# Attention and routed experts on one core: the sums of values in two PSUM banks by turns, six banks in place of seven for scores and dense stages

## The chip, the cores and the metric

The kernel runs on one core of a Trainium2 chip. The metric is the time of one launch on the device in microseconds (us), as the median of several runs. Engines are named as in the profile: PE is TensorE's matmul, PEld its weight load, DVE is VectorE, ACT is ScalarE, POOL is GpSimd, SP is SyncE, whose queue issues the DMAs.

## What is computed

The input is x of shape (2, 2048, 256). It passes two blocks, each followed by a layer norm over x plus the block's result:

```python
x = layernorm(x + windowed_attention(x))      # windows of 128, keys of the window and the one before
x = layernorm(x + ffn_block(x))
```

The second block holds most of the work. Its attention is causal over rows of x, with 16 heads of 16 columns, and its values then go to a layer of eight experts of which each row takes two:

```python
scores = einsum('bqhd,bkhd->bhqk', q, k) * scale      # q, k from x with rotary embedding
scores = where(causal, scores, -inf)
attn   = softmax(scores, axis=-1)
ctx    = einsum('bhqk,bkhd->bqhd', attn, v)
x1     = layer_norm(x + ctx @ out_proj_w.T + out_proj_b)
gates  = softmax(x1 @ gate_w.T + gate_b)              # the two largest of 8 are kept
moe    = sum over the two of gate * (x1 @ expert_w[e].T + expert_b[e])
x2     = layer_norm(x1 + moe)
```

## The kernel before

**Tiles and jobs.** The 4096 rows are 32 tiles of 128 (T in the code). The causal attention is cut into 40 jobs (J, `JOBS`): a job is four heads by two or four query tiles, and has 2 to 16 tiles of keys (`key_tiles`). For each job PE makes the scores twice. Steps `mx` (lines 1369 to 1377) put queries by keys into a PSUM bank, and DVE reduces it to row maxima (step `mr`, line 1065). From these come the negated maxima, split in three bf16 parts, transposed (`nm_T`, line 1382), copied by ACT and stored by SP as extra rows of the query operand (`nm_st`, line 806). Steps `st` (lines 1397 to 1406) then put keys by queries, with the maxima already subtracted, into a bank, and ACT takes the exponential into a ring of 16 SBUF slots (`ex`, line 978, `pbuf`). Steps `pv` (line 1424) multiply values by these exponentials, with the sums of rows as a 17th column. One `pv` step is one tile of keys, four heads beside each other on four quarters of the partitions, and it adds into one bank, `obank`, over all the key tiles of the job. Four `pv` steps of a job run without anything between them (`VRUN = 4`). After the job's last one ACT copies the bank to SBUF (`o_evac`, line 958 with `osb` as output), PE transposes it (`o_T`, line 1430), and DVE divides by the sums (`oden`, line 1109, and line 1119).

**Dense stages.** Around the jobs run, tile by tile, steps named by their first letter: `a_` for the windowed attention, `r_` for rotary embedding, projections and stores, `d_` for the output projection and norm, `f_` for the gate and the experts (`f_e0` to `f_e3` are four matmul groups of two experts each, line 1537; DVE reads `f_e0` and `f_e2` at lines 1296 and 1299, ACT reads `f_e1` and `f_e3`), `g_` for the last norms. `w_` and `load_` steps are weights and loads; `w_rows` (lines 1099 and 1100) sets a row of ones and clears `obank`.

**Banks.** PSUM has eight banks of 128 x 512 f32. Seven (`BANKS`, line 175) are shared by `mx`, `st` and every step of a dense stage that PE writes. `obank` is the eighth. Each shared bank has two semaphores, `filled[b]` and `emptied[b]`; PE waits for `emptied[b]` before the first matmul of a step, and the engine that reads the bank adds to it.

**What sets the order.** The function `plan` is a list scheduler that runs on the host when the program is built. Each step has an engine, a cost in ns, a rank (lower is more urgent) and a list of steps before it. Time after time it takes the step that can start earliest, ties by rank, gives a bank-writing step the bank that came free first, and writes down one order, which every engine's queue then follows. A kind of step can hold only so many banks at a time:

```python
BANKS = 7
SHARE = {"mx": 3, "st": 3, "stage": 4}
...
                if step[0] in EMPTIES:
                    kind = kind_of(step)
                    if not free or taken[kind] == SHARE[kind]:
                        continue
                    start = max(start, min(free)[0])
```

The first `pv` step of a run of four needs the exponentials of these four key tiles, the values of the group, and in the list `("o_evac", J - 1)`. In the program the first `pv` of job J waits with `pe.wait_ge(osb_ready, J)`, which is that the copy of the job before is done; the first job waits for the cleared bank instead.

Of the kernel before, what the change touches and what calls it, by code (L numbers as in the profile page):

```python
# [14 lines left out]
P = 128  # L15
# [4 lines left out]
DV = DH + 1  # L20
# [19 lines left out]
PB = VRUN * HJ  # L40
# [131 lines left out]

BANKS = 7
SHARE = {"mx": 3, "st": 3, "stage": 4}


# [156 lines left out]
def job_steps():  # L335

    rows = {}
    turn = [GT * place(J) + GT * (J - last_job(place(J)) - 1) / sum(place(x) == place(J) for x in range(NJ)) + GT
            for J in range(NJ)] + [GT * NG]

    def add(name, J, engine, ns, rank, *before):
        rows[name, J] = engine, ns, rank, [x for x in before if x[1] >= 0]

    for J in range(NJ):
        (s, hg, j0, nj), nk, length = JOBS[J], key_tiles(J), turn[J + 1] - turn[J]
        r, newest = turn[J], GT * s + j0 + nj - 1
        for c in range(keys_groups(J)):
            back = [("pv", J - 1, min(GT * c + GT, key_tiles(J - 1)) - 1)] if J and GT * c < key_tiles(J - 1) else [("pv_end", J - 2)]
            add(f"vload{c}", J, "SP", 500, r + 0.3 * length, ("vstore", newest), *back)
        n = len(mx_list(J))  # L350
        for i, (c, j, h, heads, cols) in enumerate(mx_list(J)):
            diag = c == s % GB
            rows["mx", J, i] = ("PE", heads * max(cols / 2.4 + 3, 98) + (220 if cols == P else 95 * heads) * diag, r + length * i / n,
                                [(f"kh{hg}{k}" if s == GB else f"kst{k}", newest) for k in range(3)] +
                                [(f"qst{k}", LATE.index(newest)) for k in range(3)])
            rows["mr", J, i] = ("DVE", heads * cols / 0.96 + 55, r + length * i / n,
                                [("mx", J, i)] + ([("nm_a", J - 1)] if J else []))
        add("nm_a", J, "DVE", 130, r - 1, ("nm_e", J - 1), *[("mr", J, i) for i in range(n)])
        for a, b in zip("bcde", "abcd"):
            add(f"nm_{a}", J, "DVE", 100, r - 1, (f"nm_{b}", J), ("nm_T", J - 1))  # L360
        add("nm_T", J, "PE", 100, r - 1, ("nm_e", J))
        add("nm_Tc", J, "ACT", 200, r - 1, ("nm_T", J), ("nm_st", J - 1))
        add("nm_st", J, "SP", 1300, r - 1, ("nm_Tc", J))
        r, n = turn[J + 1], len(st_list(J))
        for i, (kb, h, heads, cols) in enumerate(st_list(J)):
            diag = kb - first_diag(J) >= j0
            rows["st", J, i] = ("PE", heads * max(cols / 2.4 + 3, 98) + (220 if cols == P else 95 * heads) * diag, r + length * i / n,
                                [("nm_st", J), ("ones", 0)] + [("ones_later", 0)] * (s > 0))
            back = [("pv", *key_tile_at(key_tiles_before(J) + kb - VRUN))] if key_tiles_before(J) + kb >= VRUN else []
            rows["ex", J, i] = ("ACT", heads * cols * 0.833 + 68, r + length * i / n,  # L370
                                [("st", J, i)] + back + [("st0", 1), ("r_vst", 1)] * (J == i == 0))
        for kb in range(nk):

            lo, hi = st_tiles(J, kb)
            cols = (hi - lo) * P
            first, last = kb // VRUN * VRUN, min(kb // VRUN * VRUN + VRUN, nk) - 1
            rows["pv", J, kb] = ("PE", cols * 4 / 2.4 + 10 + (170 if kb == first else 0), r + length * (st_last(J, last) + 1.5) / n,
                                 [("ex", J, i) for i in range(st_last(J, last) + 1)] + [(f"vload{kb // GT}", J)] +
                                 ([("o_evac", J - 1)] if J else []) if kb == first else [("pv", J, kb - 1)])
        add("pv_end", J, "PE", 0, r + 1, ("pv", J, nk - 1))  # L380
        freed = GT * (place(J) - 2) + GT - 1
        add("o_evac", J, "ACT", 495, r + length / 2, ("pv", J, nk - 1), ("o_T", J - 1))
        add("o_T", J, "PE", 440, r + length / 2, ("o_evac", J), ("d_cT", freed))
        add("o_den", J, "DVE", 120, r + length / 2, ("o_T", J))
        add("o_ctx", J, "DVE", 340, r + length / 2, ("o_den", J), ("d_cT", freed))
    return rows
# [77 lines left out]
def build(nc, windows, cs, w_qk_t, w_out, in_t, in_b, wo_t, gate_t, exp_t, exp_b, rows, gate_b, out):  # L464
# [6 lines left out]
    with ExitStack() as ctx:  # L471
# [47 lines left out]
        vcur = sb("vcur", [P, TB, HJ, DV])  # L519
        pbuf = sb("pbuf", [P, PB, GQ])  # L520
# [5 lines left out]
        osb = sb("osb", [P, GQ])  # L526
# [74 lines left out]
        assert small_taken <= 358  # L601

        bank = [ctx.enter_context(nc.psum_tensor(f"bank{i}", [P, 512], F32)) for i in range(8)]
        obank = bank[BANKS]

        def ps(*step):
            return bank[use[step][0]]
# [16 lines left out]
        consts, rows_set, scaled = sem("consts"), sem("rows_set"), sem("scaled")  # L624
# [6 lines left out]
        osb_ready, oden_ready = sem("osb_ready"), sem("oden_ready")  # L631
# [324 lines left out]
        def _(act):  # L956
            def copy(o, i, scale=1.0):
                return nc.scalar.activation(o, i, ACT.Copy, scale=scale)  # L958

            for step in order:  # L960
# [6 lines left out]
                if name == "ex":  # L967
                    J, i = step[1:]
                    kb, h, heads, cols = st_list(J)[i]
                    nj = JOBS[J][3]  # L970
                    u0 = ((key_tiles_before(J) + kb) * HJ + h) % PB
# [13 lines left out]
                elif name == "nm_Tc":  # L985
                    J = T
# [3 lines left out]
                    nj = JOBS[J][3]  # L990
                    rows_nm = NPART * nj * HJ
                    copy(nmT[0:rows_nm, :], bk[0:rows_nm, 0:P // 2].bitcast(BF16)).then_inc(emptied[b], 1)
                elif name == "o_evac":
                    J = T
# [1 line left out]
                    if J:  # L996
                        act.wait_ge(*fill("o_T", J - 1))
                    nj = JOBS[J][3]
                    copy(osb[:, 0:nj * P], obank[:, 0:nj * P]).then_inc(osb_ready, 1)
                elif name == "a_xTc":  # L1000
                    act.wait_ge(*fill("a_xT", T))
                    copy(xT[e], bk[:, :].rearrange("p (c t) -> p c t", c=EC)).then_inc(emptied[b], 1)
# [46 lines left out]
        def _(dve):  # L1049
            v = nc.vector  # L1050
            for step in order:
# [6 lines left out]
                if name == "mr":  # L1058
                    J, i = step[1:]
                    c, j, h, heads, cols = mx_list(J)[i]  # L1060
# [7 lines left out]
                elif name == "nm_a":  # L1068
                    g, nj = keys_groups(T), JOBS[T][3]
# [7 lines left out]
                elif name in ("nm_b", "nm_c", "nm_d", "nm_e"):  # L1077
                    nj = JOBS[T][3]
# [18 lines left out]
                        v.tensor_tensor(part[2], rest, part[1], ALU.subtract).then_inc(nmp_ready, 1)  # L1097
                elif name == "w_rows":
                    v.memset(ones[:, 0, :], 1.0).then_inc(rows_set, 1)
                    v.memset(obank[:, :], 0.0).then_inc(rows_set, 1)  # L1100
                elif name == "w_scale":
                    dve.wait_ge(in_loaded, 32)
                    v.tensor_scalar(inw[:, :, 0:E], inw[:, :, 0:E], DH ** -0.5, None, ALU.mult).then_inc(scaled, 1)
# [1 line left out]
                elif name == "o_den":  # L1105
                    nj = JOBS[T][3]
# [3 lines left out]
                elif name == "o_ctx":  # L1110
                    s, hg, j0, nj = JOBS[T]
# [5 lines left out]
                    u0 = (pos % 2) * GT + j0  # L1117
# [220 lines left out]
        def _(pe):  # L1338
            mm, tr = nc.tensor.matmul, nc.tensor.transpose
            k_known = 0  # L1340
            pe.wait_ge(consts, CONSTS)
            for step in order:
# [7 lines left out]
                if name == "mx":  # L1350
                    J, i = step[1:]
                    s, hg, j0, nj = JOBS[J]
                    pos = place(J)
                    c, j, h, heads, cols = mx_list(J)[i]
# [16 lines left out]
                    for x in range(heads):  # L1371
                        head = hg * HJ + h + x
                        last = mm(bk[:, x * cols:(x + 1) * cols].rearrange("p (n t) -> p n t", t=P),  # L1373
                                  qs5[0:KR, pos % QRING, j, head, :], ks5[0:KR, kslot, 0:cols // P, head, :],
                                  start=heads < HJ, stop=x == HJ - 1 or not diag)
                        if diag and heads < HJ:
                            last = mm(bk[:, x * cols + j * P:x * cols + (j + 1) * P], idb[:, :], maskb[:, :],  # L1377
                                      start=False, stop=True)
# [4 lines left out]
                elif name == "st":  # L1383
                    J, i = step[1:]
                    s, hg, j0, nj = JOBS[J]
                    kb, h, heads, cols = st_list(J)[i]
# [12 lines left out]
                    for x in range(heads):  # L1399
                        head = hg * HJ + h + x  # L1400
                        last = mm(bk[:, x * cols:(x + 1) * cols].rearrange("p (n t) -> p n t", t=P),  # L1401
                                  ks5[0:KR + NPART, kslot, kb % GT, head, :],
                                  qs5[0:KR + NPART, place(J) % QRING, lo:hi, head, :],
                                  start=heads < HJ, stop=x == HJ - 1 or not diag)
                        if diag and heads < HJ:
                            last = mm(bk[:, x * cols:x * cols + P], maskb[:, :], idb[:, :], start=False, stop=True)  # L1406
                    last.then_inc(filled[b], 1)
                elif name == "pv":
                    J, kb = step[1:]
                    nk, nj = key_tiles(J), JOBS[J][3]  # L1410
                    lo, hi = st_tiles(J, kb)
                    r0, r1 = (lo - JOBS[J][2]) * P, nj * P
                    if kb % VRUN == 0:
                        pe.wait_ge(*drain("st", J, st_last(J, min(kb + VRUN, nk) - 1)))
                    u0 = (key_tiles_before(J) + kb) * HJ
                    if kb % GT == 0:
                        pe.wait_ge(vcur_loaded[kb // GT], 16 * (loads_before(J, kb // GT) + 1))
                    if kb == 0:
                        if J:
                            pe.wait_ge(osb_ready, J)  # L1420
                        else:
                            pe.wait_ge(rows_set, 2)
                    for h in range(HJ):
                        last = mm(obank[32 * h:32 * h + DV, r0:r1], vcur[:, kb, h, :], pbuf[:, (u0 + h) % PB, r0:r1],  # L1424
                                  start=kb == 0, stop=kb == nk - 1, tile_position=(0, 32 * h))
                    last.then_inc(pv_done, 1)
                elif name == "o_T":
                    pe.wait_ge(osb_ready, T + 1)
                    for j in range(JOBS[T][3]):
                        last = tr(bk[:, j * P:(j + 1) * P], osb[:, j * P:(j + 1) * P], idf[:, :])  # L1430
# [158 lines left out]
```

## Time and profile before

| | |
|---|---|
| median of 3 runs | 1450.21 us (1449.8 to 1451.3) |
| the profiled execution, its own time | 1447.28 us |
| its span, first to last instruction | 1445.5 us |
| PE busy | 1384.9 us, 96% |
| DVE busy | 1089.6 us, 75% |
| ACT busy | 783.6 us, 54% |
| POOL busy | 428.0 us, 30% |
| DMA queue q1, share of 16 engines | 23.2% |

The span is what the trace covers; 1.8 us of the execution lie around it. A matmul's duration in the trace holds the time until its result is written, so that two matmuls in a row overlap and a short pause between them does not show as idle time of PE. The weight load before a matmul (PEld) has a row of its own, and where a step waits for a semaphore it is most often the load that carries the wait.

### The profile page before, as it was taken

The numbers are of one execution on the slowest core, as the hardware profiler recorded it, in microseconds if no ns is written. First come the engines' busy times: TensorE is split into PE (matmuls) and PEld (weight loads), VectorE is DVE, ScalarE is ACT, GpSimd is POOL, SyncE is SP. The second block draws the span as 40 slices with busy tenths as digits, with TensorE's granted clock in tenths as the row PEclk, the third lists the DMA queues.
The fourth block names the chain that finished last, engine by engine and source line by source line (L and its number), as shares of the span: only waits on it lengthen the run. The fifth ranks groups of instructions, "written<-read, shape, count | busy, mean of one in ns | idle before, by whom it ended". The sixth has DMA issues, their size and how long they took to land.

```text
span 1445.5 us, 28119 instructions
## 1 busy us (share of the span) xinstructions
PE 1384.9 (96%) x9600; PEld 773.2 (53%) x9600; DVE 1089.6 (75%) x2736; ACT 783.6 (54%) x1707; POOL 428.0 (30%) x707
## 2 busy tenths in 40 slices
PE   7899999999999999999999999999999999999995
PEld 6767655554455445354656655555443355555542
DVE  3765877887787887778655897888778787888745
ACT  3235365555665555666655445554656467665651
POOL 4434522322232231122343543333121110111233
PEclk9999999999999999999999999999999999999997
DMA  3865422230211121120116232222120011111100
GB/s 116 201 172 128 124 57 61 58 85 21 63 46 46 38 62 33 40 57 20 50 49 156 79 90 68 57 57 65 29 60 21 22 24 29 33 32 33 34 23 12
DMA packets 152560, 88.57 MB, mean 61 GB/s; under 512 B 114430, under 2 KB 145974, under 8 KB 152163
## 3 DMA queue, kind: packets, MB, share of 16 engines
q1 hardware_dynamic: 152419, 86.78, 23.2%
q8 instruction: 78, 1.28, 0.4%
q14 instruction: 63, 0.52, 0.1%
HBM read 60.71 MB, written 25.43 MB: 60 GB/s over the span
## 4 chain that ended last, share of the span: by engine, by line
PE 44%; DVE 4%; ACT 3%; issue 2%; SPq 2%; DMA 2%; POOL 1%; POOLq 0%; DVEq 0%; ACTq 0%
PE bank L1537 11%; PE bank L1424 10%; PE bank L1401 8%; PE bank L1373 7%; ACT pbuf L978 2%; DVE mxs L1065 2%; SPq L806 1%; DMA qs<-nmT 1%; PE bank L1494 1%; PE bank L1377 1%; PE bank L1406 1%; PE bank L1513 1%; PE bank L1472 1%; PE bank L1480 1%; PE bank L1523 1%
## 5 line engine op out<-in xcount | busy, mean ns | idle before, releaser
L1065 DVE TENSOR_REDUCE mxs<-bank 128x1 f32<-128x512 f32 (+3 forms) x1120 | 709.4, 667 | 150.1 <-PE bank L1373 79.6
L978 ACT ACTIVATE pbuf<-bank 128x512 f32<-128x512 f32 (+1 forms) x1112 | 588.6, 599 | 326.1 <-PE bank L1401 151.0
L1401 PE MATMUL bank<-qs,ks 99*128 99x256 bf16 (+3 forms) x1536 | 420.7, 319 | 16.4 <-DMA qs<-nmT 10.9
L1373 PE MATMUL bank<-ks,qs 96*128 96x512 bf16 (+3 forms) x1280 | 423.0, 349 | 4.9 <-DVE mxs L1065 2.5
L1424 PE MATMUL bank<-pbuf,vcur 128*17 128x256 f32 (+3 forms) x3072 | 253.5, 469 | 0.3
L1401 PEld LDWEIGHTS bank<-qs,ks 99*128 99x128 bf16 x1536 | 142.3, 98 | 172.1 <-issue 56.3
L1537 PE MATMUL bank<-ew,x1T 128*128 128x512 f32 x464 | 222.4, 601 | 0.4 <-DVE mxs L1065 0.3
L1373 PEld LDWEIGHTS bank<-ks,qs 96*128 96x128 bf16 x1280 | 123.3, 98 | 129.7 <-issue 40.6
L1424 PEld LDWEIGHTS bank<-pbuf,vcur 128*17 128x17 f32 x3072 | 79.8, 97 | 147.4 <-issue 109.6
L1537 PEld LDWEIGHTS bank<-ew,x1T 128*128 128x128 f32 x464 | 82.0, 190 | 72.3 <-issue 60.8
L958 ACT ACTIVATE etmp<-bank,small 128x256 f32<-128x256 f32 x116 | 48.7, 471 | 80.1 <-PE bank L1537 80.1
L1377 PE MATMUL bank<-maskb,idb 128*128 128x128 bf16 x384 | 81.4, 220 | 0.0
L927 POOL TENSOR_TENSOR accp<-accp,etmp 128x256 f32<-128x256 f32 x29 | 21.1, 727 | 201.1 <-ACT etmp L958 201.1
L923 POOL TENSOR_TENSOR accp<-etmp 128x256 f32<-128x256 f32 x29 | 21.1, 728 | 188.6 <-ACT etmp L958 188.6
L1406 PE MATMUL bank<-idb,maskb 128*128 128x128 bf16 x352 | 73.6, 220 | 0.0
L1296 DVE SCALAR_TENSOR_TENSOR acc<-bank,small,acc 128x256 f32<-128x256 f32 x58 | 27.9, 480 | 52.7 <-PE bank L1537 52.7
L1494 PE MATMUL bank<-rxT,inw 128*128 128x128 f32 x464 | 57.0, 276 | 0.0
L1494 PEld LDWEIGHTS bank<-rxT,inw 128*128 128x128 f32 x464 | 55.1, 192 | 2.2 <-issue 1.3
L899 POOL CAST parts<-qkf 128x512 bf16<-128x512 f32 x28 | 17.4, 623 | 122.9 <-DVE qkf L1159 122.9
L873 POOL TENSOR_SCALAR small<-small 128x1 f32<-128x1 f32 x32 | 7.1, 223 | 156.5 <-DVE small L1143 156.3
L1377 PEld LDWEIGHTS bank<-maskb,idb 128*128 128x128 bf16 x384 | 37.8, 98 | 13.7 <-issue 8.9
L958 ACT ACTIVATE osb<-bank 128x512 f32<-128x512 f32 (+1 forms) x40 | 20.5, 512 | 43.7 <-PE bank L1424 43.1
(279 smaller groups left out, 1746.2 us busy)
## 6 DMA issues: line engine op xcount, KB each, us to landing
vcur<-v_scratch SPq DMA_DIRECT2D x92, 136.0 KB, 2.3
parts_scratch<-parts SPq DMA_DIRECT2D x29, 384.0 KB, 3.3
xw<-windows SPq DMA_DIRECT2D x29, 256.0 KB, 2.8
qs<-parts_scratch SPq DMA_DIRECT2D x32, 192.0 KB, 3.3
ks<-parts_scratch SPq DMA_DIRECT2D x28, 192.0 KB, 3.4
qs<-parts_scratch SPq DMA_DIRECT2D x32, 128.0 KB, 3.1
v_scratch<-vst SPq DMA_DIRECT2D x29, 136.0 KB, 2.4
x_scratch<-x SPq DMA_DIRECT2D x29, 128.0 KB, 1.7
```

The lines of the kernel that those rows point to most:

```text
L923: pool.tensor_tensor(accp[f], etmp[f][:, 0, :], etmp[f][:, 1, :], ALU.add).then_inc(accp1_ready, 1)
L958: return nc.scalar.activation(o, i, ACT.Copy, scale=scale)
L978: nc.scalar.activation(pbuf[:, u0:u0 + heads, nj * P - cols:nj * P], bk[:, 0:heads * cols].rearrange("p (h t) -> p h t", h=heads), ACT.Exp)\
L1065: v.reduce_max(mxs[:, j * HJ + h:j * HJ + h + heads, c], bk[:, 0:heads * cols].rearrange("p (h t) -> p h t", h=heads), AX_X)\
L1296: v.scalar_tensor_tensor(out=acc[f], in0=bk[:, 0:E], scalar=wts[f][:, 2 * k:2 * k + 1], in1=acc[f], op0=ALU.mult, op1=ALU.add).then_inc(ha ...
L1373: last = mm(bk[:, x * cols:(x + 1) * cols].rearrange("p (n t) -> p n t", t=P), qs5[0:KR, pos % QRING, j, head, :], ks5[0:KR, kslot, 0:cols ...
L1377: last = mm(bk[:, x * cols + j * P:x * cols + (j + 1) * P], idb[:, :], maskb[:, :], start=False, stop=True)
L1401: last = mm(bk[:, x * cols:(x + 1) * cols].rearrange("p (n t) -> p n t", t=P), ks5[0:KR + NPART, kslot, kb % GT, head, :], qs5[0:KR + NPAR ...
L1406: last = mm(bk[:, x * cols:x * cols + P], maskb[:, :], idb[:, :], start=False, stop=True)
L1424: last = mm(obank[32 * h:32 * h + DV, r0:r1], vcur[:, kb, h, :], pbuf[:, (u0 + h) % PB, r0:r1], start=kb == 0, stop=kb == nk - 1, tile_pos ...
L1494: last = mm(bk[:, co * P:(co + 1) * P], inw[:, ci, co * P:(co + 1) * P], rxT[e][:, ci, :], start=ci == 0, stop=ci == EC - 1)
L1537: last = mm(bk[:, :], x1T[f][:, c, :], ew[:, c, k * 2 * E:(k + 1) * 2 * E], start=c == 0, stop=c == EC - 1)
```

## The change

`BANKS` goes from 7 to 6, and the two banks left over are `obank[0]` and `obank[1]`. Job J adds its values into `obank[J % 2]`, and ACT copies from that one. The first `pv` of job J waits for the copy of job J - 2, in the planner's list and in the program (`pe.wait_ge(osb_ready, J - 1)`); jobs 0 and 1 wait for the clearing of their bank, and DVE clears two banks at the start. `SHARE` is as it was. The planner runs again with the new number and the new dependency, so that the order of all queues and the bank of each step are new.

```diff
-BANKS = 7
+BANKS = 6
 SHARE = {"mx": 3, "st": 3, "stage": 4}
...
                                  [("ex", J, i) for i in range(st_last(J, last) + 1)] + [(f"vload{kb // GT}", J)] +
-                                 ([("o_evac", J - 1)] if J else []) if kb == first else [("pv", J, kb - 1)])
+                                 ([("o_evac", J - 2)] if J > 1 else []) if kb == first else [("pv", J, kb - 1)])
...
-        obank = bank[BANKS]
+        obank = bank[BANKS:]
...
-                    copy(osb[:, 0:nj * P], obank[:, 0:nj * P]).then_inc(osb_ready, 1)
+                    copy(osb[:, 0:nj * P], obank[J % 2][:, 0:nj * P]).then_inc(osb_ready, 1)
...
-                    v.memset(obank[:, :], 0.0).then_inc(rows_set, 1)
+                    for x in obank:
+                        v.memset(x[:, :], 0.0).then_inc(rows_set, 1)
...
                     if kb == 0:
-                        if J:
-                            pe.wait_ge(osb_ready, J)
+
+                        if J >= 2:
+                            pe.wait_ge(osb_ready, J - 1)
                         else:
-                            pe.wait_ge(rows_set, 2)
+                            pe.wait_ge(rows_set, 2 + J)
                     for h in range(HJ):
-                        last = mm(obank[32 * h:32 * h + DV, r0:r1], vcur[:, kb, h, :], pbuf[:, (u0 + h) % PB, r0:r1],
+                        last = mm(obank[J % 2][32 * h:32 * h + DV, r0:r1], vcur[:, kb, h, :], pbuf[:, (u0 + h) % PB, r0:r1],
                                   start=kb == 0, stop=kb == nk - 1, tile_position=(0, 32 * h))
```

## Rows read from the trace of the kernel before

**Rows 1.** The page: span, busy time, busy PE by slice, and the clock granted.

```profile
span 1445.5 us, 28119 instructions
...
PE 1384.9 (96%) x9600; PEld 773.2 (53%) x9600; DVE 1089.6 (75%) x2736; ACT 783.6 (54%) x1707; POOL 428.0 (30%) x707
...
PE   7899999999999999999999999999999999999995
...
PEclk9999999999999999999999999999999999999997
```

**Rows 2.** The page's costliest groups (busy, mean ns, idle before and what ended it).

```profile
L1065 DVE TENSOR_REDUCE mxs<-bank 128x1 f32<-128x512 f32 (+3 forms) x1120 | 709.4, 667 | 150.1 <-PE bank L1373 79.6
L978 ACT ACTIVATE pbuf<-bank 128x512 f32<-128x512 f32 (+1 forms) x1112 | 588.6, 599 | 326.1 <-PE bank L1401 151.0
...
L1424 PE MATMUL bank<-pbuf,vcur 128*17 128x256 f32 (+3 forms) x3072 | 253.5, 469 | 0.3
...
L958 ACT ACTIVATE osb<-bank 128x512 f32<-128x512 f32 (+1 forms) x40 | 20.5, 512 | 43.7 <-PE bank L1424 43.1
```

**Rows 3.** Busy time by stretch of the span (PE, PEld, DVE, ACT, POOL, clock, DMA).

```profile
0.00:100.00 100.00, 84.31 (x596) 67.40 (x597) 60.30 (x155) 30.76 (x72) 40.97 (x79) 0.97 0.64 168
...
500.00:900.00 400.00, 391.84 (x2563) 216.68 (x2555) 302.30 (x770) 225.90 (x495) 130.13 (x210) 1.00 0.25 65
...
1000.00:1200.00 200.00, 192.91 (x1247) 86.81 (x1248) 160.53 (x384) 117.83 (x249) 38.19 (x62) 1.00 0.14 35
```

**Rows 4.** Waits of PEld between 100 and 1400 us (total us, times, longest).

```profile
PEld bank L1401 <- ACT pbuf L978: 29.6, 86, 0.5
PEld bank L1373 <- ACT pbuf L978: 21.3, 70, 0.5
PEld bank L1401 <- DVE mxs L1065: 12.3, 34, 0.6
...
PEld bank L1373 <- DVE mxs L1065: 10.9, 32, 0.7
```

**Rows 5.** Timeline, 1104.5 to 1108 us: start, duration, engine, line, operation, idle before.

```profile
1104.37 2.06 ACT L978 ACTIVATE pbuf<-bank 128x512 f32<-128x512 f32 x4
...
1104.53 0.39 PE L1373 MATMUL bank<-ks,qs 96*128 96x512 bf16 x1
1104.54 0.10 PEld L1401 LDWEIGHTS bank<-qs,ks 99*128 99x128 bf16 x1
1104.75 0.38 PE L1401 MATMUL bank<-qs,ks 99*128 99x512 bf16 x1
...
1105.01 0.10 PEld L1373 LDWEIGHTS bank<-ks,qs 96*128 96x128 bf16 x1 [0.37 <-ACT pbuf L978]
1105.01 0.39 PE L1373 MATMUL bank<-ks,qs 96*128 96x512 bf16 x1
...
1107.66 0.60 ACT L978 ACTIVATE pbuf<-bank 128x512 f32<-128x512 f32 x1 [1.23 <-PE bank L1424]
```

**Rows 6.** Timeline, 104 to 108.4 us: the shortest pause between two jobs' values.

```profile
104.07 0.84 PE L1424 MATMUL bank<-pbuf,vcur 128*17 128x256 f32 x16
...
104.99 0.38 ACT L958 ACTIVATE osb<-bank 128x256 f32<-128x256 f32 x1
...
108.18 0.41 PE L1424 MATMUL bank<-pbuf,vcur 128*17 128x256 f32 x4
```

**Rows 7.** The chain in order of time: runs of values (start, duration).

```profile
623.75 2.32 PE bank L1424 x32
643.75 3.56 PE bank L1424 x32
```

**Rows 8.** DVE between 0 and 36 us, groups by line.

```profile
L1100 DVE MEMSET bank<- 128x512 f32 x1 | 0.5, 485 | 0.1
...
L1103 DVE TENSOR_SCALAR inw<-inw 128x512 f32<-128x512 f32 x1 | 0.4, 427 | 8.5 <-DMA qkb<-in_b 8.5
```

**Rows 9.** Timeline, 1174.9 and 1214 us: a bank of `f_e0` filled and read.

```profile
1175.22 0.70 PE L1537 MATMUL bank<-ew,x1T 128*128 128x512 f32 x1
...
1214.84 0.47 DVE L1296 SCALAR_TENSOR_TENSOR acc<-bank,small,acc 128x256 f32<-128x256 f32 x1
```

## The prediction

> **What bounds the kernel now.** I read the page first. PE is busy 1384.9 of 1445.5 us, and in 37 of 40 slices its digit is 9, at a granted clock of nine tenths or more [rows 1]. So time is lost or won only where PE pauses: in the first 100 us, at the end, and in small pauses between. Next, the table of stretches: PE is busy 391.8 of 400 us between 500 and 900, and 192.9 of 200 between 1000 and 1200, where DVE has 160.5 and ACT 117.8 [rows 3]. DVE has slack on the whole, but in a stretch of scores alone it has not: the maxima of one full bank take DVE 0.67 us on average and the exponentials of one take ACT 0.60 [rows 2], while PE starts the next such fill 0.22 us after the last (1104.53 to 1104.75) [rows 5]. A pair of fills thus takes PE 0.44 us and its readers 0.6 to 0.7, so PE runs ahead until the banks are full and then waits for a reader.
>
> These waits hardly show in PE's idle time, because a matmul's row runs on past the start of the next. They show on the weight loads [rows 4]: loads of the two score lines wait for ACT's exponentials 29.6 + 21.3 us and for DVE's maxima 12.3 + 10.9, in sum 74.1 us in 86 + 70 + 34 + 32 = 222 pauses. Neither reader makes an operand of these loads; what it gives is a free bank. Part of each pause is no loss: at full pace a 0.10 us load comes every 0.22 us, so 0.12 us of idle load queue is normal. 222 x 0.12 = 26.6 us, and about 47 us of true bank waits remain. The timeline shows one: the load at 1105.01 was held 0.37 us by an exponential, and its matmul starts 0.26 us after the last, while ACT works without a pause [rows 5].
>
> **Term 1, the wait for the copy.** The change removes the wait of a job's first values for the copy of the job before. In the timeline I took the shortest pause between two jobs: values from 104.07 on, 0.84 us of them, then the copy from 104.99 to 105.37, the next job's values at 108.18 [rows 6]. The copy was done 2.8 us before anyone could have waited for it. It has to be so: the next job's first run of four wants the exponentials of four key tiles, and the last of their slots come free only with the old job's last values. A full copy is 0.6 us; the full-width jobs are further apart, as between the run at 623.75, a job's last, and the one at 643.75, the next job's first [rows 7]. All idle time of PE ahead of line 1424 is 0.3 us [rows 2]. I cost this term at 0. Its bound on the gain side is all the copies, 20.5 us [rows 2], should every one be on PE's path. There is none on the loss side: a wait on an older copy cannot end later. Nothing is queued behind it anew; the next copy waits, as before, for the transposes of the copy before.
>
> The Trainium skill says in Perfetto Trace Analysis, section Matmuls, that independent matmul groups should rotate through different PSUM banks, so that evacuation of one overlaps matmuls of the next. By that rule the two value banks would bring something here. The rows show that the overlap exists already, by other work between the jobs.
>
> **Term 2, one more clearing.** DVE clears a second bank, 0.49 us, and right behind it waits 8.5 us for the load of `in_b` [rows 8]. It is hidden: 0, or at most 0.5 us if the order puts it ahead of something urgent.
>
> **Term 3, the seventh bank.** Scores may hold three banks for maxima and three for exponentials, which is all six. With seven, one was left for a dense stage; with six, a stage that holds one takes it from the scores. What is that worth? The kernel has 100 runs of values (the key tiles of the 40 jobs, each divided by four and rounded up). A full run occupies PE for 3.56 us and a narrower one 2.32 [rows 7]; no bank is filled in it, and both readers live on what was filled before: after the run's start ACT finishes its instructions and then stands idle 1.23 us [rows 5]. One bank less is one fill less in hand at the start of every run.
> - Upper end: the reader is the limit everywhere, and each run costs one reader's instruction: 100 x 0.60 to 100 x 0.67 [rows 2], about 64 us.
> - Lower end: 0. The planner finds other steps and the loss is absorbed; by chance the new order could even be better, since any list order has some luck in it, and I let it give up to 10 us (a fifth of the 47 us of bank waits).
> - Between them: PE loses the time of the fill that it cannot do ahead, 0.22 us a run [rows 5]: 100 x 0.22 = 22 us.
> I take 22, since PE and not a reader bounds most stretches [rows 3], and what PE loses is the time in which it finds no bank. A second look at the same term: the 47 us of bank waits with seven banks would rise by 8 if they went as 7 to 6, and by 47 if they doubled. 22 is between these, too.
>
> **Sum.** 0 + 0 + 22 us on the profiled execution: 1447.28 + 22 = 1469.3. The median of the runs is 2.9 us above that execution, so 1450.2 + 22 = 1472 us. The other stages, all DMAs and the number of matmuls stay as they are. The copies' place on ACT may move, and so may `nm_st` on SP's queue; neither has a price of its own here.
>
> The Trainium skill, same page, section Matmul Optimizations, asks that all 8 banks be leveraged. Both kernels do it by count, so the rule doesn't decide; by the rows, a bank used once per job is worth less than one used by every score.
>
> **Rivals.**
> - *Faster: the copy was on the path after all.* The mechanism is term 1 at its bound. The place is the change of jobs, and it decides if the new order lets a job's first values start within 0.7 us of the last job's end (a copy starts 0.1 us after the last values and takes up to 0.6). For it: ACT stands idle 43.1 us for values before these copies [rows 2], so a copy taken off its front might let exponentials go first. Against it: the 2.8 us to spare at the narrowest place [rows 6] and 0.3 us of idle PE at line 1424. At its full price: 1450.2 - 20.5 = 1430 us; with the 10 us of a lucky order, 1440. Chance 0.14 for all of this side.
> - *Nothing much: the seventh bank was rarely needed.* The waits at the banks would then only be moved. For it: DVE and ACT are idle 25% and 46% of the span [rows 1]. Against: 222 pauses in which a bank was what was missing [rows 4]. It gives 1448 to 1457 us. Chance 0.16, of it 0.09 within 0.2% of no change.
> - *Much slower: stages hold banks for long.* The first expert group is filled at 1175.22 us and read at 1214.84, so one bank is out for 39.6 us [rows 9]; with six, scores and all other stages have five. If that makes the readers the limit, the price is the upper end: 1450.2 + 64 = 1514 us. Against it: most of the span has PE at 98%, and the planner is free to fill the experts later. Chance 0.15.
> - The forecast, a loss of some 7 to 37 us (1457 to 1487), has the remaining 0.55.
>
> **How the numbers follow.** A measurement of this kernel can tell about 0.2%, 2.9 us, from no change. Faster by more: 0.14. Within: 0.09. Slower: 0.55 + 0.15 + the 0.07 of the second rival that lies above 1453, 0.77. The range from 1446 to 1508 leaves out most of the faster side (about 0.12) and the far end of the slow one (0.06).
>
> **What would show each step.** Right: PE's busy time about as now, while the waits of loads on the score lines for lines 978 and 1065 rise from 74 us, by at least 22, with more than 222 pauses; idle PE at line 1424 stays under 1 us, and the copies are still done microseconds before the next job's values. ACT's idle time behind line 1424 grows. Wrong: if jobs' values now follow each other within a microsecond and the span falls, term 1 was mis-sized. If the load waits don't rise, term 3 is wrong, and the planner's new order absorbed the bank. If they rise by 60 us or more, and mostly at stage lines, the third rival holds.

## The result and the profile after

The changed kernel takes 1475.39 us (median of 4 runs, 1472.31 to 1478.35) against 1450.29 before (4 runs). The ratio is 1.0176, with a 95% interval of 1.0159 to 1.0193. The forecast was 1472.

The page of the changed kernel, its first and second part. The profiled execution took 1478.35 us, so its own difference to [rows 1] is 31.1 us, some 6 more than that of the medians.

```profile
span 1476.6 us, 28121 instructions
...
PE 1410.4 (96%) x9600; PEld 770.1 (52%) x9600; DVE 1095.8 (74%) x2737; ACT 790.8 (54%) x1707; POOL 427.9 (29%) x707
...
PE   7889999999999999999999999999999999999996
...
PEclk9989999999999999999999999999999999999998
```

A reader who stops at the shares sees nothing: PE is at 96% in both, and the share of every other engine is the same within a point. PE has the same 9600 matmuls, yet 25.5 us more busy time (1410.4 against 1384.9 in [rows 1]). A matmul's row is drawn longer where the next is held back for a moment or the clock is lower, so most of the new waiting counts as busy.

The costliest groups, as in [rows 2] (busy, mean ns, idle before):

```profile
L1065 DVE TENSOR_REDUCE mxs<-bank 128x1 f32<-128x512 f32 (+3 forms) x1120 | 708.8, 666 | 177.6 <-PE bank L1374 91.8
L978 ACT ACTIVATE pbuf<-bank 128x512 f32<-128x512 f32 (+1 forms) x1112 | 594.9, 595 | 361.5 <-PE bank L1402 161.4
...
L1426 PE MATMUL bank<-pbuf,vcur 128*17 128x256 f32 (+3 forms) x3072 | 253.5, 469 | 0.2 <-ACT pbuf L978 0.2
```

Neither reader works more. ACT stands idle 35 us longer before its exponentials and DVE 27 us before its maxima, and idle PE ahead of the values (line 1426, which was 1424) stays at 0.2 us.

The waits of weight loads between 100 and 1400 us, as in [rows 4] (total us, times, longest). The two score lines are now 1374 and 1402.

```profile
PEld bank L1402 <- ACT pbuf L978: 50.4, 137, 0.7
...
PEld bank L1402 <- DVE mxs L1065: 26.8, 72, 0.9
PEld bank L1374 <- ACT pbuf L978: 21.5, 68, 0.7
PEld bank L1374 <- DVE mxs L1065: 18.3, 59, 0.8
```

Here the change is in plain sight. The four rows add up to 117.0 us in 336 pauses, and before they were 74.1 us in 222. Less the 0.12 us that is normal per load, 76.7 us remain after and 47.5 before: 29 us more, beside 25 us of the medians. A pause is hardly longer than it was (0.23 us net against 0.21). There are 114 more of them. Of these, 58 begin in the last 3 us before a run of values (72 before, 130 after), and the other 56 elsewhere.

Where in the span it is lost can be read from one line's first and last start. This is line 978 before and after: its first start and its last, and below them ACT's idle time ahead of it (us, times) by what ended it.

```profile
L978 ACT ACTIVATE pbuf<-bank x1112: 484/597/778, 72.8 to 1400.9; 128x512 f32<-128x512 f32 x169, 128x384 f32<-128x384 f32 x17
...
  PE bank L1401: 151.0, 127
  PE bank L1406: 88.9, 51
  PE bank L1424: 81.4, 61
```

```profile
L978 ACT ACTIVATE pbuf<-bank x1112: 474/597/730, 77.8 to 1428.5; 128x512 f32<-128x512 f32 x169, 128x384 f32<-128x384 f32 x17
...
  PE bank L1402: 161.4, 152
  PE bank L1407: 112.7, 53
  PE bank L1426: 81.5, 61
```

The first exponential is 5.0 us later and the last 27.6, so some 23 us are lost during the jobs. The table of stretches shows the start and, in the midst of the jobs, one stretch at a lower clock (columns as in [rows 3]).

```profile
0.00:100.00 100.00, 82.36 (x532) 65.39 (x533) 59.11 (x142) 27.37 (x63) 40.98 (x79) 0.91 0.62 164
```

```profile
1118.70:1125.60 6.90, 6.90 (x18) 1.75 (x18) 5.59 (x11) 5.50 (x10) 0.83 (x2) 0.53 0.08 20
```

In the first 100 us the mean granted clock is 0.91, where it was 0.97. From 1118.7 to 1125.6 it is 0.53, so nearly all of these 6.9 us ran at the lower of the two levels (1.2 GHz), and score fills there start 0.43 us after each other:

```profile
1121.83 0.63 PE L1374 MATMUL bank<-ks,qs 96*128 96x512 bf16 x1
1122.26 0.63 PE L1402 MATMUL bank<-qs,ks 99*128 99x512 bf16 x1
1122.68 0.63 PE L1374 MATMUL bank<-ks,qs 96*128 96x512 bf16 x1
```

At the full clock it is 0.22 [rows 5]. In the 3.4 us before the clock fell, PE was busy 1.83 us: it had stood idle 1.31 us for a DMA, the stored maxima of a job (`qs<-nmT`), and 0.25 us for an exponential.

```profile
1117.14 0.38 PE L1402 MATMUL bank<-qs,ks 99*128 99x512 bf16 x1 [1.31 <-DMA qs<-nmT]
...
1118.20 0.39 PE L1402 MATMUL bank<-qs,ks 99*128 99x512 bf16 x1 [0.25 <-ACT pbuf L978]
```

The stretch costs at most half of its length, 3.4 us, and it belongs to this execution: the trace of before has a granted clock of 1.00 from 100 to 1400 us, and so has the kernel with six banks and one value bank (next section), which takes as long as the changed one. The profiled execution of before was also a quick one, 2.9 us under its median. Between the medians the clock explains little. The six-bank kernel with one value bank has a median clock of 0.990 against 0.991 for the kernel before beside it, which is worth at most 1.5 us of 27.

### The profile page after: what moved, and what is told of

It is laid out like the page before. It is cut to its first block, busy times and chain, and to the rows that moved or that the text cites. A ratio compares the mean times of both kernels' runs of the same rounds, so it can differ in the third digit from the quotient of the medians.

```text
span 1476.6 us, 28121 instructions
## 1 busy us (share of the span) xinstructions
PE 1410.4 (96%) x9600; PEld 770.1 (52%) x9600; DVE 1095.8 (74%) x2737; ACT 790.8 (54%) x1707; POOL 427.9 (29%) x707
## 4 chain that ended last, share of the span: by engine, by line
PE 42%; DVE 6%; issue 3%; ACT 2%; SPq 1%; POOL 1%; DMA 1%; POOLq 0%; DVEq 0%; ACTq 0%
PE bank L1539 10%; PE bank L1426 10%; PE bank L1402 8%; PE bank L1374 7%; DVE mxs L1065 3%; ACT pbuf L978 1%; SPq L806 1%; DMA qs<-nmT 1%; PE bank L1515 1%; PE bank L1496 1%; PE bank L1407 1%; PE bank L1378 1%; PE bank L1474 1%; PE bank L1482 1%; PE bank L1525 1%
## 5 line engine op out<-in xcount | busy, mean ns | idle before, releaser
L978 ACT ACTIVATE pbuf<-bank 128x512 f32<-128x512 f32 (+1 forms) x1112 | 594.9, 595 | 361.5 <-PE bank L1402 161.4
L1402 PEld LDWEIGHTS bank<-qs,ks 99*128 99x128 bf16 x1536 | 138.5, 98 | 209.1 <-issue 65.4
L1539 PEld LDWEIGHTS bank<-ew,x1T 128*128 128x128 f32 x464 | 81.4, 190 | 73.5 <-issue 62.3
L958 ACT ACTIVATE qT<-bank 128x256 f32<-128x256 f32 x59 | 22.6, 384 | 40.1 <-PE bank L1457 20.7
```

Of the source, the lines that this page charges most:

```text
L978: nc.scalar.activation(pbuf[:, u0:u0 + heads, nj * P - cols:nj * P], bk[:, 0:heads * cols].rearrange("p (h t) -> p h t", h=heads), ACT.Exp)\
L1539: last = mm(bk[:, :], x1T[f][:, c, :], ew[:, c, k * 2 * E:(k + 1) * 2 * E], start=c == 0, stop=c == EC - 1)
```

## The experiments

Each ran beside the kernel before on the same chip. Its ratio is to that kernel's runs there, whose median was 1449.40 to 1450.17 us.

**The lost bank without the second value bank.**

```diff
-BANKS = 7
+BANKS = 6
```

> Six shared banks, one value bank as before, the eighth bank unused. If the lost bank is the whole cost and the second value bank brings nothing, this gives the changed kernel's time, 1475 us within 4. If alternating value banks bring something and the loss of the bank is bigger than the net, this is slower than the changed kernel by that gain: 1480 or more, up to 1496 if all 20.5 us of copies counted.

1476.21 us, ratio 1.0188 (1.0162 to 1.0214). This is the changed kernel's time: the two ratios lie within each other's intervals. The whole cost is the lost bank. The comparison is a clean one, because `plan` returns the same order and the same bank for every step in both kernels: the new dependency never decided what the planner took next. What differs is the value bank, the wait before it and the second clearing. The load waits match row by row as well:

```profile
PEld bank L1401 <- ACT pbuf L978: 50.0, 137, 0.7
...
PEld bank L1401 <- DVE mxs L1065: 27.1, 72, 1.1
PEld bank L1373 <- ACT pbuf L978: 21.7, 68, 0.7
PEld bank L1373 <- DVE mxs L1065: 18.5, 59, 0.8
```

117.3 us in 336 pauses, the same number of pauses in each row. With one value bank or two, PE waits at the same places.

**Five banks.** The same edit with 5.

> Five shared banks, one value bank, two banks unused. If banks are what PE lacks, the cost grows faster than in proportion, since each run of values starts with one fill less in hand: at least 25 us more than with six, some 1510 to 1540. If the 25 us of the change were an accident of the planner's order, five need not be worse than six: 1450 to 1490.

1529.01 us, ratio 1.0552 (1.0522 to 1.0582). The seventh bank is worth 27 us and the sixth 53. The load waits on the score lines:

```profile
PEld bank L1401 <- ACT pbuf L978: 48.0, 137, 1.0
PEld bank L1373 <- ACT pbuf L978: 46.6, 118, 0.7
...
PEld bank L1401 <- DVE mxs L1065: 28.9, 88, 0.7
PEld bank L1373 <- DVE mxs L1065: 27.4, 84, 1.0
```

They are 150.9 us in 427 pauses, 99.7 net. That is 23 us more than with six banks, under half of the 53. Most of the rest stands in other rows of the same view. Over all weight loads but those of the values, the waits that ACT or DVE ended (some of them for an operand, not for a bank) are 65.5 us net with seven banks, 104.3 with six and 149.8 with five, so 39 and then 46 more. The clock has a share too: its median is 0.9865 with five banks and 0.990 with six, worth at most some 5 us.

**The six-bank order on seven real banks.** Is it PE waiting at a full bank, or an order that was planned badly?

```diff
+PLANNED = 6
...
-    free = [(0.0, b) for b in range(BANKS)]
+    free = [(0.0, b) for b in range(PLANNED)]
...
     order, use = plan()
+    use = spread(order, use)      # deals the steps of the order out over seven banks, first freed first
```

> The order is planned with six banks and one value bank, but the steps are dealt out over seven real banks in that order. If PE's waits at full banks on the chip are the cost, it goes back most of the way: 1450 to 1460, and load waits on the score lines fall to about 75 us. If the order itself is the cost (steps put where a six-bank plan wants them), it stays at 1468 to 1478.

1451.88 us, ratio 1.0020 (1.0009 to 1.0031). With the order of the six-bank kernel and one real bank more, nearly all is back. In this kernel the lines are 15 higher:

```profile
PEld bank L1416 <- DVE mxs L1080: 22.9, 61, 0.8
PEld bank L1388 <- DVE mxs L1080: 22.8, 62, 0.9
PEld bank L1388 <- ACT pbuf L993: 19.7, 67, 0.5
PEld bank L1416 <- ACT pbuf L993: 15.7, 49, 0.4
```

81.1 us in 239 pauses, near the 74.1 in 222 of before. So the order planned for six banks is nearly as good as the one planned for seven, and the cost is the waiting for banks on the chip.

The plan has this cost as well. By the planner's own costs of the steps, PE's queue ends at 1474.2 us with seven banks, 1504.9 with six and 1553.5 with five: 31 and then 49 us more, where the chip took 27 and 53. This is a computation and no measurement, but it needs nothing except the number of banks and how long each reader takes.

**The copy later, in the kernel before.** ACT rewrites the value bank in place before it copies it.

```diff
+                    copy(obank[:, 0:nj * P], obank[:, 0:nj * P]).then_inc(again, 1)
+                    act.wait_ge(again, J + 1)
                     copy(osb[:, 0:nj * P], obank[:, 0:nj * P]).then_inc(osb_ready, 1)
```

> The kernel before, with the release of the next job's values made later: at each of the 40 jobs ACT first rewrites the value bank in place and then copies it to SBUF, so that the release comes some 0.5 to 0.7 us later. If the copy is on PE's path between jobs, the time grows by all of it, about 20 to 26 us. If it is not, by 0 to 6 us, what ACT's 20 us of extra work cost where ACT limits, and idle PE ahead of line 1424 stays near 0.3 us.

1456.54 us, ratio 1.0047 (1.0030 to 1.0064), 6.6 us more, at the edge of what was expected off the path. The added instructions and the values' own row:

```profile
L959 ACT ACTIVATE bank<-bank 128x512 f32<-128x512 f32 (+1 forms) x40 | 19.9, 497 | 43.7 <-PE bank L1427 43.1
```

```profile
L1427 PE MATMUL bank<-pbuf,vcur 128*17 128x256 f32 (+3 forms) x3072 | 253.5, 469 | 0.3
```

The release of the next job's values came at least 19.9 us later in sum, and PE's idle time ahead of them is 0.3 us as before. The order of all steps is that of the kernel before, so luck of an order has no part in the 6.6 us. Where most of them can come from shows at another step. The copy also releases the transpose of the job's values (`o_T`, here line 1433), and PE now stands idle for the copy ahead of it, which it does nowhere in the kernel before (total us, times, longest).

```profile
PE bank L1433 <- ACT osb L959: 4.8, 14, 0.4
```

**A pool of eight.** All eight banks are shared. A job's values take one from their first step to the copy, and between two jobs it serves scores and stages.

```diff
-BANKS = 7
-SHARE = {"mx": 3, "st": 3, "stage": 4}
+BANKS = 8
+SHARE = {"mx": 3, "st": 3, "stage": 4, "pv": 1}
...
-                if step[0] in EMPTIES:
+                if step[0] in EMPTIES or step[0] == "pv" and step[2] == 0:
...
-                        last = mm(obank[32 * h:32 * h + DV, r0:r1], ...
+                        last = mm(bank[use["pv", J, 0][0]][32 * h:32 * h + DV, r0:r1], ...
```

> All eight banks in one pool; a job's values take one of them from their first step to the copy, and between jobs it is free for scores and stages. One value bank at a time, the order of jobs' values as before. If banks are what PE lacks, this gives some of what an eighth shared bank would: 5 to 15 us faster than before, 1435 to 1445. If seven are enough and only the sixth-to-seventh step costs, no change: 1447 to 1453.

1442.53 us, ratio 0.9949 (0.9930 to 0.9967): faster than both kernels. The four rows of load waits:

```profile
PEld bank L1400 <- ACT pbuf L977: 21.7, 72, 0.4
PEld bank L1400 <- DVE mxs L1065: 11.3, 29, 0.9
...
PEld bank L1372 <- DVE mxs L1065: 10.4, 30, 1.0
PEld bank L1372 <- ACT pbuf L977: 9.7, 29, 0.5
```

They fall to 53.1 us in 160 pauses, 33.9 net. PE's idle time ahead of the values is 2.2 us in this kernel. In its program a job's values wait only until the bank that they take is free, and 34 of the 39 jobs after the first take another bank than the job before them. So the values of this kernel already change banks from job to job.

**The pool with turns.** As above, with `"pv": 2` and the dependency on the copy of job J - 2.

> The same pool of eight, but two jobs' values may hold a bank each and a job's first values wait only for the copy of the job before the last. This is the alternation without a bank given up for it. If alternation brings nothing, it is within 3 us of the pool with one value bank. If the copy's wait costs something that the lost bank hid, it is 5 to 20 us faster than that.

1443.02 us, ratio 0.9953 (0.9936 to 0.9969). The intervals of the two pools nearly coincide, and they must: `plan` returns the same order and banks for both, and their programs are the same instruction for instruction. The run shows how well a time repeats and that this planner has no use for turns. It is no second measurement of what turns are worth on the chip.

**The pool with four and four.** `SHARE` with `"mx": 4, "st": 4`.

> The pool of eight with one value bank, and shares of four banks for maxima and four for exponentials in place of three and three. If the caps keep PE from using the banks that are there, a further 3 to 8 us against the pool with three and three: 1435 to 1440. If three in hand are enough for each reader, no change: 1441 to 1445; if stages are then short of banks, slower than 1446.

1442.80 us, ratio 0.9945 (0.9925 to 0.9966). No change in the time: the caps are not what holds the pool back.

**The first expert group later.** This is for the third rival, banks that a stage holds for long. Once in the kernel before, once in the changed one:

```diff
-        add("f_e0", T, "PE", 1720, ("d_x1Tc", T))
+        add("f_e0", T, "PE", 1720, ("d_x1Tc", T), ("f_wT", T))
```

> The kernel before, with the first expert group planned only once the gate's weights are transposed, so that its bank is not held for up to 40 us. If long-held stage banks are part of what makes banks scarce, a gain of 3 to 12 us: 1438 to 1447. If the scores' own banks are the limit, no change, or a few us of loss, since PE has one filler less: 1448 to 1455.

> The changed kernel, with the first expert group planned only once the gate's weights are transposed. If banks held long by a stage are the cost of going to six (one of five left for scores), it wins back 10 us or more of the 25: 1455 to 1465. If the loss is in the scores' own turnover, it stays at 1470 to 1478.

With seven banks 1462.02 us, ratio 1.0080 (1.0060 to 1.0100); with six 1486.38, ratio 1.0246 (1.0223 to 1.0269). They are 12 and 11 us slower than their own base. Both theories missed this. The edit did what it was meant to do: the time from the first matmul of `f_e0` to its reader, summed over the 32 tiles, falls from 333 to 143 us with seven banks and from 304 to 77 with six. In the first of the two the load waits on the score lines did fall as well:

```profile
PEld bank L1401 <- ACT pbuf L978: 22.9, 70, 0.4
PEld bank L1373 <- ACT pbuf L978: 15.4, 52, 0.5
PEld bank L1401 <- DVE mxs L1065: 14.6, 37, 0.8
...
PEld bank L1373 <- DVE mxs L1065: 7.2, 29, 0.5
```

In sum they are 60.1 us in 188 pauses, 74.1 in 222 in [rows 4]. So fewer bank waits are no gain by themselves. Why the time grew isn't shown. It may be that early matmuls had filled pauses of PE, whose idle time went from 60.6 to 68.4 us. But these two kernels also ran at a lower clock than any other with as many banks (medians of 0.9845 and 0.9835 against 0.990 and 0.991 for the kernel before beside them), worth at most 8 and 11 us, and each is a single order. Since shorter holding won nothing back with six banks, the long-held bank is not what makes the step from seven to six dear.

**Other orders of the same kernels.** One number of the planner is shifted: the settling time of DVE's results, 150 ns, becomes 140 or 170.

```diff
-SETTLE = {"PE": 200, "ACT": 150, "DVE": 150, "POOL": 120, "SP": 1700}
+SETTLE = {"PE": 200, "ACT": 150, "DVE": 140, "POOL": 120, "SP": 1700}
```

> The kernel before with another order of about the same quality: the planner is told that DVE's results settle in 140 ns, not 150. This measures how much the time moves by the luck of an order. If the 25 us are banks and not luck, this is within 6 us of before, 1444 to 1456. If orders scatter by 20 us, it need not be.

> The kernel before with DVE's settling time planned at 170 ns, a second other order with seven banks. Banks: 1444 to 1458. Luck: anywhere from 1440 to 1475.

> The changed kernel with the same small shift of the planner (140 ns). Banks: within 6 us of the changed kernel, 1469 to 1481. Luck: it may fall anywhere from 1450 to 1490.

With seven banks 1446.46 us (0.9976, 0.9961 to 0.9991) and 1456.07 (1.0041, 1.0024 to 1.0058); with six, two value banks, 1473.69 (1.0158, 1.0133 to 1.0184). Orders of one kernel scatter by 10 us. The three orders with seven banks end at 1456.07, those with six begin at 1473.69; luck doesn't bridge that. Even the kernel with seven banks and the late expert group, at 1462.02, stays under it. The scatter also tells how little half a per cent of a planned kernel means. The pool's gain of 7 us is of its size, though both pool orders (three and three, four and four) gave it alike.

## Why the prediction was right, and where it was not

**Term 1, the copy's wait, cost at 0: right, shown twice.** With the lost bank alone, and the same order, the time is the same as with the turns as well; and a release made 0.5 us later per job left idle PE ahead of the values at 0.3 us. Over the 39 changes of jobs the least time from the end of a copy to the next values is 2.8 us, in the kernel before and in the changed one. There it looks as in [rows 6]:

```profile
110.28 0.62 PE L1426 MATMUL bank<-pbuf,vcur 128*17 128x256 f32 x12
...
110.96 0.38 ACT L958 ACTIVATE osb<-bank 128x256 f32<-128x256 f32 x1 [0.16 <-PE bank L1426]
...
114.16 0.62 PE L1426 MATMUL bank<-pbuf,vcur 128*17 128x256 f32 x8
```

The copy ends at 111.34 and the next values start 2.8 us later. Neither the planner nor the chip used the freedom that the second bank gave.

**Term 2, a second clearing at 0.** No run had it alone. The kernel with six banks and one value bank doesn't have it, has the same order, and is not faster than the changed one, so it is within the noise.

**Term 3, the seventh bank, 22 us: the size right, 25 us for the medians; its working half right.** I priced it as one fill less in hand at the start of each of 100 runs of values. Where the pauses fall bears out a part of it: the last 3 us before a run have 58 of the 114 new pauses and 18 of the 43 us, the rest of the span the others, for which the working has no term. About one fill time for each of 114 pauses and 0.22 us for each of 100 runs give the same size, and that the second came so near the measured time is in part luck. The second look, by the load waits of [rows 4], needed no such picture; their net rise of 29 us lies between its two bounds of 8 and 47.

Of the signs that the prediction named, two failed. PE's busy time was to stay about as now and grew by 25.5 us, since pauses hide inside the rows of matmuls, as the prediction itself had said. And ACT's idle time behind the values was to grow. It is 81.4 us in 61 waits before and 81.5 in 61 after. That came from a wrong reading of [rows 5]. I took ACT's 1.23 us there for a lack of filled banks. But in the kernel the exponential of a new key tile waits for `pv_done`, until a `pv` step has freed its slots in the ring `pbuf`, and by the trace a filled score bank already stood ready when 54 of these 61 waits began (41 of the 61 after). A bank more or less can't shorten such a wait. What grew is ACT's idle time behind score matmuls, 161.4 + 112.7 against 151.0 + 88.9.

**The rivals.** *Faster* fell with term 1. *Nothing much* fell with the load waits; what it got right is that the order planned for six banks is hardly worse. *Much slower by long-held banks* fell too: its price was 64 us, and it set out from the longest hold of all, 39.6 us. On average a bank of `f_e0` is held for 10 us, and holding it for less won nothing back.

**Not foreseen:** the clock. In the profiled executions it was lower at the start (0.91 against 0.97) and once in the middle. Between the medians its share is small, and it is not shown that waits for banks lowered it; the pause before the stretch in the middle was mostly one for a DMA.

**Left open:** which part of the 11 and 12 us with the late expert group is the clock, the lost filler or the luck of an order; and the 2 us of the slower copy's 6.6 that PE's waits for the transposes do not cover.

## What to carry to other kernels

Before giving an accumulator a second buffer, look at how long after its copy the next accumulation starts; here the copy had 2.8 us to spare, and a second buffer was worth nothing. In this kernel a bank shared by the operations of every microsecond was worth far more than one that changes hands 40 times in a launch, and the second one taken away cost more than the first (27 us, then 53). A buffer that is dedicated only part of the time can go into the common pool for the rest: here this gave 7 us, no more than orders scatter. And where a planner makes the order, let it plan the change before you run it: here it used no turns, and its own time said 31 us for a loss of 27.

## What the runs showed that I had not expected

- The order planned for six banks ran on seven real banks within 0.2% of the order planned for seven. How many banks the planner knows of matters less than one bank more on the chip.
- Making the first expert group hold its bank less long [rows 9] brought no gain but a loss of 11 to 12 us, with six banks as with seven. Why is open.
- A planner constant moved by 10 or 20 ns moved the time by 4 and 6 us, with no operation changed.
